# First batch's query tiles between its key steps, Newton scratch of the keys in PSUM, queries normalised by GpSimd, second input prepared slot by slot

## What is computed

```python
xn = layernorm(layernorm(x)); q = xn @ Wq; k, v = split(xn @ Wkv)      # 16 heads, 4 groups, 64 wide
q, k = layernorm(q) * qn_scale + qn_bias, layernorm(k) * kn_scale + kn_bias    # per head
out = softmax(q k^T / 8) v; x = x + out @ Wout                         # per batch, 4 heads share a group
```

## Time and profile before

| | |
|---|---|
| median of three runs | 911.64 us |
| the profiled execution | 914.55 us, span of its instructions 912.8 us |
| mean granted TensorE clock | 0.964 |
| first batch: prologue and production, attention | to 102, to 382 us (its last slot ends inside the next prologue) |
| second batch: prologue and production, attention | to 461, to 751 us |
| the other three blocks | to 912.8 us |

### The profile page before, as it was taken

The page is one execution under the profiler, slowest core; times in us unless marked ns, Lnnn a source line. Parts: engine busy times, 40 slices in busy tenths (PEclk is TensorE's granted clock), DMA queues, the critical chain, the costliest instruction groups (busy, mean ns, idle before and its releaser), DMA issues. The chain is left out here.

```text
span 912.8 us, 13410 instructions
## 1 busy us (share of the span) xinstructions
PE 842.0 (92%) x4860; PEld 447.7 (49%) x4860; DVE 632.7 (69%) x1072; ACT 456.2 (50%) x822; POOL 541.6 (59%) x319
## 2 busy tenths in 40 slices
PE   2697899999999999979799999999999964999998
PEld 2454444454445444544344454445444432568675
DVE  6877677777777777378767777777777637155772
...
DMA packets 49596, 7.98 MB, mean 9 GB/s; under 512 B 42486, under 2 KB 47994, under 8 KB 49530
## 3 DMA queue, kind: packets, MB, share of 16 engines
...
...
## 5 line engine op out<-in xcount | busy, mean ns | idle before, releaser
L399 POOL TENSOR_TENSOR space<-space 128x1024 f32<-128x1024 f32 x160 | 380.2, 2376 | 39.9 <-ACT space L752 22.2
L975 DVE TENSOR_REDUCE part<-psum 128x2 f32<-128x1024 f32 x256 | 313.3, 1224 | 122.6 <-PE psum L511 119.1
L752 ACT ACTIVATE space<-psum 128x512 f32<-128x512 f32 x512 | 264.6, 602 | 154.3 <-PE psum L531 150.0
L546 PE MATMUL psum<-space,vb 128*64 128x512 f32 x1024 | 249.1, 608 | 0.0
L511 PE MATMUL psum<-kh,qh 64*128 64x512 f32 x512 | 129.2, 501 | 13.4 <-DVE part L975 13.4
L404 POOL TENSOR_TENSOR space<-space 128x1024 f32<-128x1024 f32 x30 | 71.5, 2384 | 100.2 <-DVE space L991 100.2
L511 PEld LDWEIGHTS psum<-kh,qh 64*128 64x128 f32 x512 | 48.3, 185 | 147.3 <-DVE part L975 111.0
L546 PEld LDWEIGHTS psum<-space,vb 128*64 128x64 f32 x1024 | 62.6, 137 | 108.0 <-issue 72.7
L531 PE MATMUL psum<-qh,kh 64*128 64x512 f32 x512 | 103.4, 399 | 0.0
L531 PE MATMUL psum<-ql,kh 64*128 64x512 f32 x512 | 102.8, 396 | 0.0
L531 PE MATMUL psum<-qh,kl 64*128 64x512 f32 x512 | 102.4, 394 | 0.0
(11 more groups left out here) (160 smaller groups left out, 871.7 us busy)
## 6 DMA issues: line engine op xcount, KB each, us to landing
ql<-nmx SPq DMA_DIRECT2D x256, 0.5 KB, 2.0
...
```

Source lines behind the costliest of these rows:

```text
L399: pool.tensor_tensor(to, pt[0] if u == 1 else to, pt[u], ALU.add)\
L546: last = pe.matmul(outp[rows(h), :], vb[:, place(m)[1], kt, :], pt[kt][:, h, :], start=(kt == 0), stop=(kt == TILES - 1))
L752: act.activation(pt[kt][:, h, :], key_scores[kt % 2][h], ACT.Exp).then_inc(exp_made, 1)
L975: dve.tensor_reduce(to[:, half, :], scores.rearrange("p (h k) -> p h k", h=2), AX_X, ALU.max, negate=True)\
```

## The change

- The first batch's key steps and query tiles 0 to 3 are one list on each engine; key steps 2 and 3 use PSUM banks 6 and 7. Key/value step 2 stands ahead of the first transposes. The same for the second batch, behind key step 3. `produce` begins with tile 4 in both.
- The sums of the keys' squares and the scratch of their Newton step lie in the value bank of the step; the sum therefore waits for the copied values.
- VectorE writes the normalised keys once and GpSimd copies them to their twin place (`twin`); the transposes wait for that.
- All queries are normalised by GpSimd (`normal`), from the copy of ScalarE, which now copies all eight tiles.
- GpSimd's products with the weights wait for the shift vector; the first twins stand between them.
- At the end of `produce` the first maxima of slot 1 and the first key scores and exponents of slot 0 stand ahead of the last query tiles; phase 5 of VectorE is in there.
- The second batch's x: VectorE's statistics one tile per phase from phase 20, the rest in phase 28; GpSimd's root and shift behind slot 8; ScalarE normalises a tile per phase from phase 48; PE transposes in phase 64, ScalarE keeps it in phase 65.
- Between the batches the key sum of step 2 stands ahead of the last slot's corrections, the last addition behind the keys of step 3, and PE's wait for that addition ahead of the first query transposes.

Cut to its core (eight columns of indent are off; ScalarE's second list goes the same way as its first):

```diff
-def kv_at(s):
-    return [banks(2 + 2 * (s % 2) + i, 1) for i in range(2)]
+def kv_at(b, s):
+    first = (2, 4, 6, 6) if b == 0 else (2, 4, 2, 4)
+    return [banks(first[s] + i, 1) for i in range(2)]
+def key_sums(b, s):
+    scratch = kv_at(b, s)[1]
+    return scratch[:, 0:2 * GROUPS], scratch[:, 2 * GROUPS:4 * GROUPS]
...
+    def scale_first():
         pool.wait_ge(cross_made, 1)
         pool.wait_ge(wq_centred, 1)
+        pool.wait_ge(shift_made, 1)
         pool.tensor_tensor(folding, centred, over_mid(cross[:, 2, :], HEADS), ALU.mult).then_inc(scaled_made, 1)
+    def scale_rest():
         pool.tensor_tensor(folded, centred, over_mid(cross[:, 0, :], HEADS), ALU.mult).then_inc(scaled_made, 1)
-        pool.wait_ge(firsts_made, 1)
+    def take_first():
+        pool.wait_ge(firsts_made, 2)
         link(pool.tensor_tensor(folded, folded, over_last(firsts[:, 1, :], DH), ALU.subtract))
         pool.tensor_scalar(folded[:, :, 0], firsts[:, 0, :], 1.0, 0.0, ALU.mult, ALU.add).then_inc(w_folded, 1)
-    def normalise(b):
-        pool.wait_ge(root_made, b + 1)
-        for j in range(TILES):
-            last = pool.tensor_scalar(xn[b][:, j, :], x[:, b, j, :], mv[:, j, 0:1], st[:, b, 1, j:j + 1], ALU.subtract, ALU.mult)
-        last.then_inc(xn_made[b], 1)
+    def twin(b, s):
+        pool.wait_ge(kn_made, STEPS * b + s + 1)
+        pool.tensor_scalar(kn[s % 2][:, :, 1, :], kn[s % 2][:, :, 0, :], 1.0, 0.0, ALU.mult, ALU.add).then_inc(twin_made, 1)
...
+    def normal(b, j):
+        n = TILES * b + j
+        rate(j, n)
+        pool.wait_ge(u_kept, n + 1)
+        if j >= 2:
+            pool.wait_ge(q_turned, n - 1)
+        pool.tensor_tensor(qn[j % 2].rearrange("p (h d) -> p h d", d=DH), u_kept_at[j % 2], over_last(q_rate[:, j % 2, 4, :], DH), ALU.mult)\
+            .then_inc(qn_made, 1)
...
+    def shift_x(b):
+        pool.wait_ge(root_made, b + 1)
+        link(pool.tensor_tensor(st[:, b, 2, :], mv[:, :, 0], st[:, b, 1, :], ALU.mult))
+        pool.tensor_scalar(st[:, b, 2, :], st[:, b, 2, :], -1.0, 0.0, ALU.mult, ALU.add).then_inc(shift_x_made, 1)
...
-    fold()
+    scale_first()
+    twin(0, 0)
+    scale_rest()
+    twin(0, 1)
+    take_first()
+    twin(0, 2)
+    normal(0, 0)
     pool.wait_ge(r_in, 16 * N_RAW)
     pool.tensor_scalar(raw[:, W_GATE * P:], rawi[:, :], SCALE1, 0.0, ALU.mult, ALU.add).then_inc(w_float, 1)
-    root(1)
-    normalise(1)
+    twin(0, 3)
...
+        if b:
+            for s in range(STEPS):
+                twin(b, s)
+            normal(b, 0)
+        for j in range(1, TILES):
+            normal(b, j)
...
+            if n == SLOTS // 2:
+                root(1)
+                shift_x(1)
...
-        pe.wait_ge(kn_made, n + 1)
+        pe.wait_ge(twin_made, n + 1)
...
+        elif b:
+            pe.wait_ge(x_added, SLOTS * b)
+        else:
+            pe.wait_ge(kn_made, STEPS)
+            pe.wait_ge(v_made, STEPS)
...
+            if b == 0 and ph == 4 * SLOTS:
+                pe.wait_ge(part_made, 8 * SLOTS)
+                pe.wait_ge(xn_made[1], TILES)
+                turn_x(1, 0, TILES)
...
-        for j in range(TILES):
+        for j in range(T, TILES):
             norms(b, j)
-            if j == 0:
-                turn_keys(b, STEPS - 1)
-            if j >= DIRECT:
-                unit_scores(SLOTS * b, 2 * (j - DIRECT))
-            if j >= 2:
-                turn_queries(b, j - 2)
+            unit_scores(SLOTS * b, 2 * (j - T))
+            turn_queries(b, j - 2)
             folded(b, j)
-            extra(j)
-            if j >= DIRECT:
-                unit_scores(SLOTS * b, 2 * (j - DIRECT) + 1)
+            unit_scores(SLOTS * b, 2 * (j - T) + 1)
         turn_queries(b, TILES - 2)
         unit_scores(SLOTS * b + 1, 0)
         unit_scores(SLOTS * b + 1, 1)
+        tile_scores(SLOTS * b, 0)
+        tile_scores(SLOTS * b, 1)
         turn_queries(b, TILES - 1)
...
     keys_values(0, 0)
     keys_values(0, 1)
+    keys_values(0, 2)
     turn_keys(0, 0)
-    keys_values(0, 2)
+    norms(0, 0)
     turn_keys(0, 1)
+    folded(0, 0)
     keys_values(0, 3)
+    norms(0, 1)
     turn_keys(0, 2)
+    folded(0, 1)
+    norms(0, 2)
+    turn_keys(0, 3)
+    folded(0, 2)
+    turn_queries(0, 0)
+    pe.wait_ge(w_float, 1)
+    pe.wait_ge(kh_made, STEPS)
+    pe.wait_ge(kl_made, STEPS)
+    turn_w(0, 8)
+    norms(0, 3)
+    turn_queries(0, 1)
+    folded(0, 3)
+    pe.wait_ge(w_kept, 1)
+    turn_w(8, W_TILES)
     produce(0)
     attention(0, 4 * SLOTS + LAG + 1)
+    pe.wait_ge(xnt_made, 3)
     keys_values(1, 0)
     keys_values(1, 1)
     add_up(SLOTS - 1)
     turn_keys(1, 0)
     keys_values(1, 2)
     turn_keys(1, 1)
+    keys_values(1, 3)
     project_out(SLOTS - 1)
-    keys_values(1, 3)
     turn_keys(1, 2)
-    pe.wait_ge(x_added, SLOTS)
+    norms(1, 0)
+    folded(1, 0)
+    turn_keys(1, 3)
+    norms(1, 1)
+    folded(1, 1)
+    norms(1, 2)
+    turn_queries(1, 0)
+    folded(1, 2)
+    norms(1, 3)
+    turn_queries(1, 1)
+    folded(1, 3)
     produce(1)
     attention(1, 4 * SLOTS + LAG + 9)
...
+        if n >= 2:
+            act.wait_ge(qn_made, n - 1)
...
         high_queries(b, TILES - 2)
+        exps(SLOTS * b, 0)
+        exps(SLOTS * b, 1)
         high_queries(b, TILES - 1)
...
+            if b == 0 and 0 <= ph - 4 * (SLOTS - 4) < TILES:
+                j = ph - 4 * (SLOTS - 4)
+                act.wait_ge(shift_x_made, 1)
+                act.activation(xn[1][:, j, :], x[:, 1, j, :], ACT.Identity, bias=st[:, 1, 2, j:j + 1], scale=st[:, 1, 1, j:j + 1])\
+                    .then_inc(xn_made[1], 1)
             m, k = divmod(ph - LAG, 4)
-            if m < SLOTS:
+            if m < SLOTS and ph > LAG:
                 exps(SLOTS * b + m, 2 * k)
                 exps(SLOTS * b + m, 2 * k + 1)
+            if b == 0 and ph == 4 * SLOTS + 1:
+                act.wait_ge(xn_turned, 3)
+                keep_x(1, 0, TILES)
...
-    for s in range(STEPS):
-        square_keys(0, s)
-        keep_values(0, s)
-        guess_keys(0, s)
-        if s:
-            high_keys(0, s - 1)
+    square_keys(0, 0)
+    keep_values(0, 0)
+    guess_keys(0, 0)
+    square_keys(0, 1)
+    keep_values(0, 1)
+    guess_keys(0, 1)
+    square_keys(0, 2)
+    keep_values(0, 2)
+    high_keys(0, 0)
+    square_queries(0, 0)
+    guess_keys(0, 2)
+    high_keys(0, 1)
+    keep_folded(0, 0)
+    guess_queries(0, 0)
+    square_keys(0, 3)
+    keep_values(0, 3)
+    guess_keys(0, 3)
+    square_queries(0, 1)
+    high_keys(0, 2)
+    keep_folded(0, 1)
+    guess_queries(0, 1)
+    square_queries(0, 2)
+    high_keys(0, 3)
+    keep_folded(0, 2)
+    guess_queries(0, 2)
+    high_queries(0, 0)
+    act.wait_ge(w_turned, 1)
+    keep_w(0, 8)
+    square_queries(0, 3)
+    high_queries(0, 1)
+    keep_folded(0, 3)
+    guess_queries(0, 3)
+    act.wait_ge(w_turned, 2)
+    keep_w(8, W_TILES)
     produce(0)
     attention(0, 4 * SLOTS + LAG + 1)
     act.wait_ge(pv_made, TILES * (SLOTS - 1) + 2)
...
+        dve.wait_ge(v_made, n + 1)
+        dve.tensor_reduce(key_sums(b, s)[0], ksq[s % 2].rearrange("p (h d) -> p h d", d=DH), AX_X, ALU.add).then_inc(ksum_made, 1)
...
-        newton(k_rate[:, s % 2])
+        total, t = key_sums(b, s)
+        guess, r = k_rate[:, s % 2, 1, :], k_rate[:, s % 2, 2, :]
+        link(dve.scalar_tensor_tensor(out=t, in0=total, scalar=DH * ATT_EPS, in1=guess, op0=ALU.add, op1=ALU.mult))
+        link(dve.scalar_tensor_tensor(out=t, in0=t, scalar=-0.5 / DH, in1=guess, op0=ALU.mult, op1=ALU.mult))
+        link(dve.scalar_tensor_tensor(out=r, in0=t, scalar=1.5, in1=guess, op0=ALU.add, op1=ALU.mult))
         if s >= 2:
             dve.wait_ge(k_turned, n - 1)
-        pairs = [P, 2 * GROUPS, 2, DH - 1]
-        dve.tensor_tensor(kn[s % 2][:, :, :, 1:], kv_at(s)[0].rearrange("p (h d) -> p h d", d=DH)[:, :, 1:].unsqueeze(2).broadcast_to(pairs),
-                          k_rate[:, s % 2, 4, :].unsqueeze(2).unsqueeze(3).broadcast_to(pairs), ALU.mult).then_inc(kn_made, 1)
+        dve.tensor_tensor(kn[s % 2][:, :, 0, 1:], kv_at(b, s)[0].rearrange("p (h d) -> p h d", d=DH)[:, :, 1:],
+                          over_last(k_rate[:, s % 2, 2, :], DH - 1), ALU.mult).then_inc(kn_made, 1)
...
+            largest(SLOTS * b, 2 * (j - T))
+            low_queries(b, j - 2)
+            largest(SLOTS * b, 2 * (j - T) + 1)
+        largest(SLOTS * b + 1, 0)
         low_queries(b, TILES - 2)
-        largest(SLOTS * b + 1, 0)
         largest(SLOTS * b + 1, 1)
+        largest(SLOTS * b + 1, 2)
         low_queries(b, TILES - 1)
+        largest(SLOTS * b + 1, 3)
...
+            if b == 0 and 0 <= ph - 4 * 5 < TILES:
+                dve.bn_stats(stats[:, ph - 4 * 5, :], x[:, 1, ph - 4 * 5, :]).then_inc(x_stats, 1)
+            if b == 0 and ph == 4 * 7:
+                dve.wait_ge(x_stats, TILES)
+                aggregate(0, TILES)
+                variances(1)
...
     normal_keys(0, 1)
+    sum_keys(0, 2)
+    first_sums()
```

(21 more changed lines are left out.)

160 lines of the change are left out of this document (59 added, 101 removed).

## The result

| | before | changed |
|---|---|---|
| median of 7 runs each | 912.33 us | 905.84 us |
| ratio, 95% interval | | 0.9932 [0.9914, 0.9951] |
| a second set (11 and 6 runs) | 912.08 us | 906.63 us, 0.9940 [0.9918, 0.9961] |
| profiled execution, span | 914.55, 912.8 us | 907.61, 905.8 us |

What follows compares the result with a forecast made beforehand. TensorE was taken as busy 842 of 912.8 us, with the holes in both prologues, where engines hand work on. Terms -7.6 -1.9 +2.3 -1.5 -2.2 gave -10.9, so a median of 900.7 us, range 896.0 to 907.5.

Steps and rivals of the forecast that it cites:

- Prologue of the first batch, -7.6: First batch, up to the projection of query tile 4: it starts at 51.0 us, 7.6 earlier; bounds 3.8 to 9.
- The rival that gave the scratch no effect: Key steps: Newton steps 1 and 2 still wait for GpSimd, 1.6 and 1.9 us; whole 904.2 us, chance 0.07.
- Normalising by GpSimd: Query tiles: a pass takes 1.90 us against VectorE's 1.22, but is never last in the first batch.
- The slower rival: First prologue: new holes bring half clock, 25 us of PE work doubles, +21 us; whole 921.7 us, chance 0.06.
- End of production, -1.9 and -2.2: Ends of both batches: phase 6 starts 12.3 us after folded tile 7, 1.9 and 2.2 us earlier than before.
- I keep the old lengths: End of production: phase 6 was assumed to keep its lengths, 6.8 us in the first batch and 5.46 in the second.
- Clock stays up: Rival, ends of production: phase 6 lasts 4.1 us, 2.7 and 1.3 more saved; whole 896.7 us, chance 0.10.
- Attention of the first batch, +2.3: Preparing the second input there costs 2.3 us: transposes 1.04, statistics and aggregation 1.0, ScalarE 0.2, GpSimd's root covered.
- Second prologue, -1.5: Second batch, up to the projection of query tile 4: it starts at 417.3 us, 1.5 earlier (0 to 3).
- Sum: Whole kernel: the terms -7.6, -1.9, +2.3, -1.5 and -2.2 add to -10.9 us.
- 905.25: Rival, both prologues: hand-offs between engines eat half, leaving gains of 3.8 and 0.75 us; whole 905.25 us, chance 0.18.
- 906.8: Rival, first batch's attention: it pays in full for the second input, 8.4 us and not 2.3; whole 906.8, chance 0.09.

Runs made afterwards that it cites:

- again: The changed kernel run once more, unchanged, as a second set with its own profile; ratio to before 0.9940.
- n_sbuf: The changed kernel with the key sums and the Newton scratch back in SBUF, every wait kept; ratio to before 0.9971.
- q_dve: The changed kernel with Newton steps and multiplication of query tiles 0 to 3 back on VectorE, in both batches; ratio to before 0.9935.
- p_order: The changed kernel with the first batch's lists undone on every engine, four key steps first, then query tiles 0 to 3; ratio to before 0.9922.
- t_old: The changed kernel with the old order at the end of production put back in both batches; ratio to before 0.9921.
- s_nowait: The changed kernel without GpSimd's wait for the query shifts before its first product of the weights; ratio to before 0.9923.

## Why the prediction came out as it did

- **Prologue of the first batch, -7.6:** -6.6 in the profile, -5.7 with as much half clock as before (-6.4 in "rest"), and 36.4 to 37.2 us long in six executions without any. Tile 4 was forecast at 51.0 and came at 51.5, which is partly luck: in those six it started at 48.5 to 49.3. I had added durations of 1.88 and 1.04 where the starts are 1.72 and 0.87 apart, and half clock and slow first records made up for it. Put back one at a time, "rest" grew by 3.5 for the queries (1.6 of it half clock), 1.2 for the order, 1.0 for the scratch, 0.7 for the twins and 0.3 for GpSimd's wait. The order is read against the changed kernel's first profile, the others against `again`; these are single profiles, and their sum is 6.7, near the 6.4. The rival that gave the scratch no effect, 3.5 us at chance 0.07, named the two stalls (1.6 and 1.9), and n_sbuf measured them (1.70 and 1.73 over the usual 0.17), but the path lost only 1.0. The PSUM steps took 0.17, not my 0.2. So the errata rule of the Trainium skill (VectorE: DVE Perf Modes, The TRN2 errata), 65 ns more for each, doesn't show in these rows: a step is 0.17 us with either source.
- **Normalising by GpSimd:** the Trainium skill's rule (GPSIMD Engine Reference, 4.1 Engine selection) speaks against it, and here the move pays: a pass takes 1.90 against 1.22 us, 1.56 times and not twice, and yet q_dve, with four of the tiles back on VectorE, has P2 0.3 us longer and "rest" 3.5.
- **The slower rival, half clock in the prologue:** real, but small. 6.8 us of it stood in the changed kernel's second profile and cost 2.6 us in "rest" (3.4 us cost 1.2 in the first), not 21, for only the work inside slowed.
- **End of production, -1.9 and -2.2: the step that failed.** -0.7 and +0.3 in the profile. Over the 16 ends with this order (eight profiles) E averages 19.2, over the four with the old one 19.9, but at like half clock the means of the two orders differ by 0.1 us: the new end as such was worth next to nothing. Phase 6 came at F+12.2 to F+12.3 in five of the 16, as worked out, at F+13.3 to 14.7 in the others: I had counted the key scores at full clock (1.4 us) behind a gap that can bring half clock (2.6). And "I keep the old lengths" failed: phase 6 takes 4.1 us at full clock and up to 6.8 at half, so what is won ahead of it can be lost inside it. With 6.8 us of half clock each, E1 of p_order has phase 6 at F+12.2 and t_old's at F+14.7, phase 7 at F+18.5 and F+18.8. The idle VectorE (3.14 us, and 1.64 in `again` at full clock) was in my times, as the third unit score stood behind key scores and transposes; I didn't ask whether it had to. "Clock stays up" did come in E1 of two profiles (`again` and s_nowait: 4.1 us for phase 6, E1 16.4).
- **Attention of the first batch, +2.3:** +2.1, the right sum of partly wrong terms. Transposes 1.04 against 1.02, aggregation 0.7 against 0.62; the statistics' 0.3 was 0, ScalarE's 0.2 was 0, and the root, which I had covered with GpSimd's 3.3 us wait, cost 0.40: it was issued behind the addition that ends that wait, not ahead of it.
- **Second prologue, -1.5:** -3.2. Transposes 2 ended at +16.6 us from the first projection as forecast (16.7), but the full stretch behind it took 17.1, not 18.6: I added durations of 1.88 and 1.04 where records overlap and the starts are 1.72 and 0.87 apart. Of the 3.2, twins on GpSimd are 1.0, queries 0.3 and the scratch nothing (35.43 in n_sbuf); the rest, by difference the lists, wasn't tried alone.
- **Sum.** Profile to profile the forecast missed by 3.9 (-10.9 against -7.0): 3.6 in the two ends (-4.1 against -0.5), 1.0 in P1, 1.3 in the unchanged rest, less 1.7 in P2 and some 0.3 in small terms. Another 0.8 lies between the two profiles and the ratio of all runs. The measured 905.8 lies by the numbers of three rivals (905.25, 904.2, 906.8), and none of them came true: the prologues gave 6.6 and 3.2 and not half, the scratch works, the attention paid 2.1. Open is how far before's own P1 and ends swing, as there is one profile of it, 2.9 us over its first median.
